# Moving VectorE, TensorE, ScalarE and GpSimd work inside the batch loop of a GAT and GRU graph kernel

## What is computed

```python
h = jnp.maximum(_layernorm(x), 0.0)                  # x: 8 batches, 1024 nodes, 128 features
x = x + gat(h, adj, W, a)                            # attention over the graph, then elu
h = jnp.maximum(_layernorm(x), 0.0)
x = x + gated_graph(h, adj, weight, w_ih, w_hh, b_ih, b_hh)

# gat:  e[i,j] = leaky(e_i[i] + e_j[j]), masked where adj is 0, softmax over j, times h W
# gated_graph, for each of 3 layers:
m = h @ weight[i];  aggr = A.T @ m                   # A = (adj != 0)
r = sigmoid(i_r + h_r);  z = sigmoid(i_z + h_z);  n = tanh(i_n + r * h_n)
h = (1 - z) * n + z * h                              # i_* from aggr, h_* from h
```

## Time and profile before

| | |
|---|---|
| median of the runs | 689.55 us |
| the profiled execution | 689.75 us, of which its span 687.9 us |
| busy: PE, DVE, ACT, POOL | 91%, 78%, 66%, 37% of the span |
| longest waits of POOL | 172.9 us for z from ACT, 146.9 and 52.4 us for statistics from DVE |
| ACT's exp for the maximum from DVE | 47.1 us in 33 waits |
| distance of one body from the next | 80.4 us |
| mean granted clock of PE | 0.984 |

### The profile page before, as it was taken

One profiled execution on the slowest core, in us unless ns is written; L12 is line 12 of the kernel. 1 busy time (PEld: TensorE's weight loads), 2 busy tenths in 40 slices (PEclk: granted clock), 3 DMA queues, 4 the chain that ended last, 5 costly groups with the idle time before them and its releaser, 6 DMA issues.

```text
span 687.9 us, 8791 instructions
## 1 busy us (share of the span) xinstructions
PE 623.6 (91%) x2845; PEld 458.4 (67%) x2845; DVE 539.0 (78%) x1234; ACT 451.9 (66%) x777; POOL 255.4 (37%) x263
## 2 busy tenths in 40 slices
PE   2686999998999899998999989998999999999995
PEld 2465776676686676776766766766767776767774
DVE  4767998599876998779985998769987699648545
ACT  2784787477874778566875778647785677554443
POOL 1203544246241461525432453414715234413440
PEclk9799899999999999999999999999999999999998
DMA  6521131023202132022410132021320122001001
GB/s 222 183 93 62 62 121 32 33 61 123 92 31 92 33 123 92 15 79 61 146 39 32 62 123 92 30 81 44 122 93 6 56 87 67 1 1 30 1 1 30
DMA packets 28669, 47.39 MB, mean 69 GB/s; under 512 B 1672, under 2 KB 19408, under 8 KB 28624
## 3 DMA queue, kind: packets, MB, share of 16 engines
q1 hardware_dynamic: 28624, 46.84, 21.0%
HBM read 42.60 MB, written 4.23 MB: 68 GB/s over the span
## 4 chain that ended last, share of the span: by engine, by line
PE 55%; DVE 26%; ACT 8%; issue 5%; POOL 5%; DMA 1%; DVEq 0%; ACTq 0%; POOLq 0%
PE ps_x L970 14%; PE ps_g L1008 10%; PE ps_x L951 6%; DVE score L665 5%; DVE zh L757 3%; ACT score L389 3%; PE ps_r L1017 2%; DVE zh L764 2%; PE ps_z L1018 2%; PE ps_z L1017 2%; PE ps_r L1019 2%; PE ps_r L1018 2%; PE ps_z L1019 2%; DVE hkT L751 2%; DVE nn L744 2%
## 5 line engine op out<-in xcount | busy, mean ns | idle before, releaser
L1008 PE MATMUL ps_g<-edges,h_hi 128*128 128x512 f32 x384 | 157.7, 411 | 10.6 <-DVE h_lo L773 9.2
L1008 PE MATMUL ps_g<-edges,h_lo 128*128 128x512 f32 x384 | 152.2, 396 | 0.0
L389 ACT ACTIVATE score<-score,nmax 128x1024 f32<-128x1024 f32 x64 | 73.8, 1153 | 48.1 <-DVE nmax L665 47.1
L970 PE MATMUL ps_x<-probT,h_nat 128*128 128x512 f32 x224 | 98.9, 594 | 0.0
L1008 PEld LDWEIGHTS ps_g<-edges,h_hi 128*128 128x128 f32 x384 | 73.1, 190 | 29.0 <-DVE h_lo L773 12.8
L665 DVE CUSTOM_DVE_ANT_0 score<-score,away 128x1024 f32<-128x1024 f32 x64 | 86.6, 1353 | 7.3 <-ACT score L383 6.5
L300 POOL TENSOR_SCALAR tz<-tz 128x512 f32<-128x512 f32 x32 | 24.6, 769 | 172.9 <-ACT tz L430 172.9
L275 POOL TENSOR_SCALAR rstd<-mv 128x4 f32<-128x4 f32 (+1 forms) x24 | 9.9, 412 | 199.4 <-DVE mv L707 146.9
L1008 PEld LDWEIGHTS ps_g<-edges,h_lo 128*128 128x128 f32 x384 | 73.2, 191 | 14.0
L396 ACT ACTIVATE probT<-ps_x 128x512 f32<-128x512 f32 x128 | 70.9, 595 | 17.2 <-PE ps_x L951 17.1
L951 PE MATMUL ps_x<-ident,score 128*128 128x128 f32 x512 | 71.0, 281 | 11.4 <-ACT score L389 10.0
(11 more groups left out here) (136 smaller groups left out, 1331.5 us busy)
## 6 DMA issues: line engine op xcount, KB each, us to landing
adj_in<-in_adj SPq DMA_DIRECT2D x64, 512.0 KB, 3.3
x_nat<-in_x SPq DMA_DIRECT2D x8, 512.0 KB, 4.3
ej<-ej_kept_at SPq DMA_DIRECT2D x8, 512.0 KB, 3.4
out<-nn SPq DMA_DIRECT2D x16, 256.0 KB, 2.3
probT<-in_L_gnn_weight SPq DMA_DIRECT2D x1, 192.0 KB
probT<-in_L_gnn_w_ih SPq DMA_DIRECT2D x1, 192.0 KB
probT<-in_L_gnn_w_hh SPq DMA_DIRECT2D x1, 192.0 KB
ej_kept_at<-ej_row SPq DMA_DIRECT2D x8, 4.0 KB
```

Of the source, the lines that this page charges most:

```text
L389: act.activation(score[t % U][:], score[t % U][:], ACT.Exp, bias=nmax[:, t:t + 1], scale=-1.0, accum_out=rowsum[:, t:t + 1]).then_inc(exp_ ...
L970: last = pe.matmul(bank_of("agg", c, par)[:], h_nat[par][:, j, :], probT[:, j, :], start=(j == 0), stop=(j == T - 1))
L1008: last = pe.matmul(ps_g[c][:], part[:, s, :], edges[par][:, s, cols(c)], start=(s == 0 and part is h_hi), stop=(s == T - 1 and part is h_lo))
```

## The change

Nothing is added or taken away; the same operations stand in other places.

1. DVE, layer 0: `g_lo_half(b, 0, 0)` stands between the two `out_half`, where `away_tile(a, 1)` was, and `g_lo_half(b, 0, 1)` behind `scores(a, 1)`. `away_tile(a, 1)` goes to the end of the body before. `n_input(b, 0, 0)` stands ahead of `away_tile(a, 2)` and `scores(a, 2)`, where it was behind them. The edges of tiles 0 to 2 go behind; `lo_half(b, 0, 0)` goes between the two operations of `n_input(b, 0, 1)`.
2. `norm1(b + 2)` goes from the start of the body to layer 1, behind `n_input(b, 1, 0)`; POOL's `rstd1(b + 2)` from the start of the body to between the two `z_times_h` of layer 1; ACT's `h_tiles` and DVE's `dots` from layer 1 to its end and to layer 2.
3. PE, layer 0: the products of z with h stand ahead of those of r; hn waits for the first `out_half` alone and r for the second. `probT_tile(a, 0)` goes ahead of `h_back(b - 1, 2, 1)`. `h_back(b, 0, 0)` goes into `gates_g(b, 0, 1)`, ahead of its products for `ps_in`. In `early_neighbours(1)` the `h_back` of half 1 stands four products later.

```diff
DVE
-                if attend:
-                    away_tile(a, a_par, 1)
+                g_lo_half(b, 0, 0)
                 if b > 0:
                     out_half(b - 1, a_par, 1)
                 if attend:
                     scores(a, 1)
-                if prepare:
-                    norm1(b + 2, par)
-                g_lo_half(b, 0, 0)
                 g_lo_half(b, 0, 1)
...
+                n_input(b, 0, 0)
+                if attend:
                     away_tile(a, a_par, 2)
                     scores(a, 2)
-                n_input(b, 0, 0)
+                new_h(b, 0, 0)
...
                 n_input(b, 1, 0)
+                if prepare:
+                    norm1(b + 2, par)
                 new_h(b, 1, 0)
...
-                if prepare:
-                    dots(b + 2, par)
...
                 g_lo_half(b, 2, 1)
+                if prepare:
+                    dots_ej(b + 2)
                 if attend:
                     split_h0(a, 0)
                 if prepare:
+                    dots_ei(b + 2, par)
                     away_tile(b + 2, par, 0)
+                    away_tile(b + 2, par, 1)
PE
-                if l == 0 and c == 0:
-                    pe.wait_ge(out_done, b * 2 + 1)
+                if l == 0 and c == 0 and b > 0:
+                    pe.wait_ge(out_done, b * 2)
...
+                if l == 0 and c == 0:
+                    product(ps_z[:], whh(1), h, True, False)
+                    if b > 0:
+                        pe.wait_ge(out_done, b * 2 + 1)
                 product(ps_r[:], whh(0), h, True, False)
...
                 product(ps_z[:], of_g(1), g, False, True).then_inc(z_ps, 1)
+                if l == 0 and c == 1:
+                    h_back(b, 0, 0)
                 if c == 1:
                     pe.wait_ge(pre_done, n - 1)
                 product(ps_in[:], of_g(2), g, True, True).then_inc(in_ps, 1)
...
+                    neighbours(b, par, l, 0, 1, range(0, TH // 2))
                     h_back(b, l - 1, 1)
-                    neighbours(b, par, l, 0, 1)
+                    neighbours(b, par, l, 0, 1, range(TH // 2, TH))
```

More of the change, by code:

```diff
@@ L326, in body @@
             def body(b, par, attend, prepare):
-                if prepare:
-                    rstd1(b + 2)
                 for l in range(L - 1):
                     z_times_h(b, l, 0)
+                    if prepare and l == 1:
+                        rstd1(b + 2)
                     z_times_h(b, l, 1)
@@ L507, in body @@
                     leaky_tile(a, a_par, 4)
-                if prepare:
-                    h_tiles(b + 2, par, 0)
                 if attend:
@@ L525, in body @@
                     leaky_tile(a, a_par, 6)
-                if prepare:
-                    h_tiles(b + 2, par, 1)
-                if attend:
                     exp_tile(a, 6)
@@ L541, in body @@
                     leaky_tile(a, a_par, 7)
+                if prepare:
+                    h_tiles(b + 2, par, 0)
                 hi_half(b, 1, 1)
@@ L553, in body @@
                 g_hi_half(b, 2, 1)
+                if prepare:
+                    h_tiles(b + 2, par, 1)
                 if attend:
@@ L633, in dots, with dots_ej @@
             def dots(b, par):
+                dots_ej(b)
+                dots_ei(b, par)
+            def dots_ej(b):
                 dve.wait_ge(h_done, b * 2 + 2)
@@ L639, in dots, with dots_ei, dots_of @@
                     dve.wait_ge(ej_ps, b)
[L640 to L644, removed]
+                dots_of(b, b % 2, 1, ej_col)
+            def dots_ei(b, par):
+                dots_of(b, par, 0, ei[par])
+            def dots_of(b, par, k, dst):
+                for t in range(T):
+                    last = dve.scalar_tensor_tensor(dot[:, k, t, :], h_nat[par][:, t, :], 1.0, w_rep[:, k, :], ALU.mult,
+                                                    ALU.mult, accum_out=dst[:, t:t + 1])
+                last.then_inc(e_done, 1)
             def away_tile(b, par, t):
@@ L726, in n_input, with r_times_hn @@
             def n_input(b, l, c):
+                r_times_hn(b, l, c)
+                add_in(b, l, c)
+            def r_times_hn(b, l, c):
                 n = b * QS + 2 * l + c + 1
@@ L730, in n_input, with add_in @@
                 dve.scalar_tensor_tensor(pre[c][:], tr[c][:], 1.0, hnb[c][:], ALU.add, ALU.mult).then_inc(rh_done, 1)
+            def add_in(b, l, c):
+                n = b * QS + 2 * l + c + 1
                 dve.wait_ge(rh_done, n)
@@ L804, in first @@
                 away_tile(1, 1, 0)
+                away_tile(1, 1, 1)
             def body(b, par, attend, prepare):
@@ L818, in body @@
                     scores(a, 1)
-                if prepare:
-                    norm1(b + 2, par)
-                g_lo_half(b, 0, 0)
                 g_lo_half(b, 0, 1)
+                n_input(b, 0, 0)
+                if attend:
+                    away_tile(a, a_par, 2)
+                    scores(a, 2)
+                new_h(b, 0, 0)
                 if attend:
                     edge_tile(a, a_par, 0)
-                    away_tile(a, a_par, 2)
-                    scores(a, 2)
-                n_input(b, 0, 0)
+                r_times_hn(b, 0, 1)
+                lo_half(b, 0, 0)
+                add_in(b, 0, 1)
                 if attend:
                     edge_tile(a, a_par, 1)
[L830 to L834, removed]
                 new_h(b, 0, 1)
@@ L837, in body @@
                     away_tile(a, a_par, 3)
+                    edge_tile(a, a_par, 2)
                 lo_half(b, 0, 1)
                 if attend:
+                    scores(a, 3)
                     edge_tile(a, a_par, 3)
-                    scores(a, 3)
                     away_tile(a, a_par, 4)
@@ L1046, in rz_of_h @@
                     pe.wait_ge(tz_done, n - 1)
-                product(ps_z[:], whh(1), h, True, False)
+                if l > 0 or c == 1:
+                    product(ps_z[:], whh(1), h, True, False)
             def gates_h(b, l, c):
@@ L1117, in body @@
                 neighbours(b, par, 0, 1, 1)
+                if attend:
+                    probT_tile(a, a_par, 0)
                 if b > 0:
                     h_back(b - 1, 2, 1)
-                if attend:
-                    probT_tile(a, a_par, 0)
                 gates_h(b, 0, 0)
@@ L1127, in body @@
                 gates_g(b, 0, 1)
-                h_back(b, 0, 0)
                 if attend:
```

1 line of the change is left out of this document (removed).

## The result

The changed kernel took 713.62 us, the median of four runs (712.78 to 714.31); the kernel before took 689.5 us (689.12 to 689.65) in the same session. The ratio is 1.035, with a 95% interval of 1.0332 to 1.0368: slower, by 24.1 us. The forecast was 711.5 us.

What follows compares the result with a forecast made beforehand. The prediction took the chain, more than half PE and a quarter DVE, as the bound. Terms 14.5 + 5.1 + 3.0 - 0.5 = 22.1 us on 689.75 gave 711.9, named 711.5 us; range 694 to 721.

Steps and rivals of the forecast that it cites:

- The meeting with POOL: Layer 0, half 0: DVE's scores of tile 2 run beside POOL's product z times h, 1.1 to 1.2 us more.
- The second meeting: Layer 0: DVE's new_h(0, 1) meets POOL's zh and split of half 0 once or twice, each 0.5 to 1.2 us.
- Half 1: Layer 0: hkT of half 1 at 253.4 to 254.6, late neighbours starting at 255.4 to 256.8, not 253.87.
- Layer 1: The statistics moved into DVE's wait there delay hnb(1, 1): 0.2 us a body, bounds 0 and 0.5.
- The clock: PE's granted clock drops behind its 4.4 us wait at h_back(0, 0): 0.9 us a body, bounds 0 to 2.
- Layer 0: Layer 1's gates start 1.2 to 2.6 us later in each body because of the new order in layer 0.
- 2.9 a body: Loss taken for each of bodies 1 to 5 from layer 0, layer 1 and the clock; 14.5 us for the five.
- Body 0: Statistics already under idle time, but the same queue behind: loses 3.0 us (1.5 to 4).
- Body 6: Has no statistics, was quicker before by 2.2 us and loses this as well: 5.1 us.
- Body 7: Has no scores; hn starts and h_lo comes sooner: -0.5 us (-1.3 to 0).
- The outer bounds: Whole kernel: all low bounds 1.4 a body, +10.8, 700 us; all high ones 4.3 a body, +32, 721 us.
- Rival 2: Bodies 1 to 5 do as well as body 6 without statistics in layer 0: -11, 678 us; chance 0.08.

Runs made afterwards that it cites:

- the exchange alone: The kernel before with only n_input(b, 0, 0) put ahead of away and scores of tile 2 on DVE; 708.58 us, ratio 1.0278.
- the last run: The kernel with the new start and old middle of layer 0, with the early neighbours of half 1 unsplit on PE; 679.86 us, ratio 0.986.
- the first run: The changed kernel with away and scores of tile 2 ahead of n_input(b, 0, 0) on DVE again; 685.98 us, ratio 0.9952.

## Why the prediction was right, and where a term was off

The mechanism was right up to the late hkT of half 0 and its size; behind it two terms were off and cancelled. In the frame of before:

- DVE waits for r until 240.08 (named 240.05, "2.9 us", measured 2.83); the scores of tile 2 end at 244.3 (244.4); n_gate runs at 245.52 (245.65); h_back(0, 0) at 247.80 ("until 247.8"). The two neighbouring runs show it as a cause: scores first takes away 27.6 us, and the exchange alone gives 19 to the kernel before.
- *The meeting with POOL.* Named 1.1 to 1.2, measured 0.98 for the scores; moved apart, it gives back 7.3 us of seven bodies. The second meeting struck too: hkT(0, 1) took 1.68 us, where it took 0.98 before. The Trainium skill, "GPSIMD Engine Reference", section "Key points", says that DVE's instructions with two SBUF inputs, as these two have, contend with POOL; these runs agree and give the size.
- *Half 1.* Late neighbours at 263.27 - 6.68 = 256.59, named 255.4 to 256.8.
- *Layer 1, "I take 0.2".* Nearly right: 0.1 here. The statistics were put where DVE waited, and h_back(1, 0) stands 282.06 - 240.44 = 41.62 us behind the frame, 39.15 before; layer 0 had already lost 2.4 of these 2.5 (layer 1's gates 260.38 for 257.94). In the run with the statistics alone, where half 0 comes in time, they cost 0.3. DVE's row of the changed kernel behind them has no wait left:

```profile
273.61 1.63 DVE L623 BATCH_NORM_STATS2 stats<-x_nat 128x6 f32<-128x128 f32 x8
275.28 0.64 DVE L629 BATCH_NORM_AGGREGATE mv<-stats 128x2 f32<-128x6 f32 x8
275.84 0.66 DVE L760 SCALAR_TENSOR_TENSOR nn<-tz,nn 128x512 f32<-128x512 f32 x1
```

- *The clock, "some 0.9 of it stays".* Mis-sized, the largest miss among the terms. The clock fell to its lower level, 1.2 GHz, behind the wait in all of bodies 1 to 5 (0.50 to 0.67 granted over the 3 to 5 us behind it), but it cost 0.2 us a body on the mean: where it is short, the slow stretch lies before the late neighbours, which wait for hkT of half 1 and so for ACT and DVE. "TensorE: Matmul & The Clock Gate" of the Trainium skill, section "HAM oscillation — how this bites in real kernels", was right for this kernel that the clock would be put back in turn after turn, though not in body 0; what that costs is a matter of the path.
- *Layer 0, "+1.2 to +2.6".* Too low in the value taken, about 1.8 (2.9 less 0.2 and 0.9). With the clock at 1.00 (the run with PE kept busy) a body is 2.65 us longer than before: 2.3 by PE's first product of hn in layer 1 (27.35 us behind the frame for 25.04), both meetings having struck in full, 0.1 in layer 1 and 0.2 behind it, where I had named 0 to 0.1. So the right 2.9 a body was in part luck, two errors that cancelled: bodies 1 to 5 gave (565.10 - 148.63) - (546.65 - 144.54) = 14.36, named 14.5.
- *Body 0, 3.0*: 3.4. *Body 6, 5.1*: 4.5. *Body 7, "-0.5"*: wrong in sign, +0.47. h_lo did come sooner, PE's wait for it was 0.71 us where it was 1.41. But the split of the early neighbours, which I had costed nowhere, took 0.8 of it back, as the last run shows, and the new order of half 1 another 0.6 (52.65 for 52.09 us, the first run against that with the old half 1).
- Some 0.7 us more is setup, and not of the change: DVE's last h_hi there, ahead of every row of DVE that moved, starts at 69.69 for 68.99, and between 68.66 and 70.58 in the other runs.
- *The outer bounds* were added up wrongly. The terms' own bounds give 1.2 and 2.6 + 0.5 + 2 = 5.1 us a body, not 1.4 and 4.3; the high side of the range would have been about 726 and not 721.
- Rival 2 ("faster", 678) had its premise right and its condition wrong. The statistics in layer 0 did cost about 2 us a body, and without the rest of the change one gets 678.66; the scores of tile 2 had to stay ahead.

So the sum of the parts, taken in this order from 689.5, is: statistics -10.8; the away in setup, the new start and the split +2.6; edges and scores of tile 3 in their new order +4.5 to 4.7; n_input ahead of the scores of tile 2 +27.6 to 27.8; together +24.1. The third is a difference of runs in which several rows moved; which of them counts wasn't tried. The parts don't simply add in any order: the last one cost 19 in the kernel before.

## What to carry to other kernels

When one operation is put ahead of another in an in-order queue, look at what the first one waits for, and whose queue stands behind the second: here DVE idled 2.83 us for r in front of 1.2 us of ready work on which ACT, and through ACT the hurried operation itself, depended. The thing to order by is the whole cycle through both queues: the scores fit into the wait for r for nothing, and a wait on POOL that kept it out of DVE's way paid for itself. Cost a moved block by the wait into which it goes (the statistics, 2.3 us of DVE's time, cost 0.1 to 0.3), and take a mixed change apart, since its good half can be hidden by the other.

## What the runs showed of the hardware

- The same wait doesn't always bring the clock down. In the run with POOL's product behind the scores PE waited 3.14 or 3.15 us at h_back(0, 0) in bodies 1 to 6. The granted clock fell behind it in five of them; in body 3 it stayed at 1.00 (335 to 355 us). Nor does it fall at the same point: rows of bodies 1, 3 and 6, with 1.11 us for four transposes at the lower clock and 0.66 at the full one:

```profile
170.75 1.11 PE L971 MATMUL ps_hn<-ident,hkT 128*128 128x128 f32 x4 [3.14 <-DVE hkT L769]
...
335.78 0.66 PE L971 MATMUL ps_hn<-ident,hkT 128*128 128x128 f32 x4 [3.15 <-DVE hkT L769]
...
582.14 0.66 PE L971 MATMUL ps_hn<-ident,hkT 128*128 128x128 f32 x4 [3.15 <-DVE hkT L769]
```

  In body 6 the transposes still ran at the full clock, and it was 0.50 over 584 to 586: full speed in the first row behind a wait doesn't show that the clock held. Shorter waits did it too: one of 2.65 us, with exp(2) behind n_gate, in bodies 3 to 6 and not in 1 and 2. In the changed kernel 3.13 us in body 0 left the clock at 1.00 (84 to 94), and 4.11 or 4.12 us brought it down in bodies 1 to 6.
- A DVE instruction and a POOL instruction that meet can both get longer: DVE 1.22 to 2.20 and POOL 1.26 to 1.83 in one meeting.
